# Second attention stage of a two-layer kernel: the second of GpSimd's two row gathers is issued behind the three rounding passes

## What is computed

```python
x = x + tanh(g_xattn[0]) * L0_xattn(layernorm(x), ctx)   # 8 heads of 64
x = x + tanh(g_ffn[0])   * L0_ffn(layernorm(x))          # 16 experts, best 2 of each token
x = x + tanh(g_xattn[1]) * L1_xattn(layernorm(x), ctx)   # 16 heads of 8
x = x + tanh(g_ffn[1])   * L1_ffn(layernorm(x))          # x rounded to fp8, times an fp8 kernel
```

## Time and profile before

| | |
|---|---|
| runs | 1152.71, 1152.83, 1156.85 us, median 1152.83 |
| profiled execution | 1153.63 us, of which the span shown is 1151.9 us |
| busy over the span | PE 90%, PEld 73%, DVE 71%, POOL 56%, ACT 51% |
| stage C | from some 710 us to the end |
| steps 12 to 17 | from 773.16 to 817.47 us |

### The profile page before, as it was taken

The page is one execution under the profiler, slowest core; times in us unless marked ns, Lnnn a source line. Parts: engine busy times, 40 slices in busy tenths (PEclk is TensorE's granted clock), DMA queues, the critical chain, the costliest instruction groups (busy, mean ns, idle before and its releaser), DMA issues. The chain is left out here.

```text
span 1151.9 us, 40516 instructions
## 1 busy us (share of the span) xinstructions
PE 1035.9 (90%) x13498; PEld 844.1 (73%) x13498; DVE 814.5 (71%) x2572; ACT 590.3 (51%) x1415; POOL 650.7 (56%) x1155
## 2 busy tenths in 40 slices
PE   4999999996999997499949996888999999899993
PEld 3787878774777775288848985666788888788882
DVE  1777777776777775655525555577899999799984
ACT  2666666662666564144515442234556555465554
POOL 1333333232777777566663545447777777577656
PEclk9999999997999999599979998799999999899997
DMA  3412112331334300144424543111111111111101
GB/s 76 90 42 52 42 38 61 91 75 40 92 95 108 98 25 27 55 139 140 134 74 130 144 137 89 30 30 29 32 38 37 32 37 38 30 37 34 33 24 31
DMA packets 106902, 74.39 MB, mean 65 GB/s; under 512 B 21360, under 2 KB 98288, under 8 KB 106736
## 3 DMA queue, kind: packets, MB, share of 16 engines
q1 hardware_dynamic: 98544, 55.40, 18.5%
q0 software_dynamic: 8192, 16.79, 4.9%
HBM read 38.60 MB, written 33.55 MB: 63 GB/s over the span
## 5 line engine op out<-in xcount | busy, mean ns | idle before, releaser
L678 ACT ACTIVATE arena<-PS 77x512 f32<-77x512 f32 (+4 forms) x736 | 303.9, 439 | 424.7 <-PE PS L1194 288.4
L1194 PE MATMUL PS<-arena 128*32 128x128 f32 (+5 forms) x9488 | 452.0, 292 | 36.6 <-DMA logit_bias<-in_bias 12.7
L1194 PEld LDWEIGHTS PS<-arena 128*32 128x32 f32 (+4 forms) x9488 | 352.5, 147 | 114.4 <-ACT arena L678 29.1
L604 POOL DMA_INDIRECT moe_in<-moe_results,slot x128 | 130.5, 1020 | 129.1 <-PE PS L1194 63.0
L1194 PE MATMUL PS<-w,arena 128*128 x960 | 192.4, 319 | 2.2 <-ACT arena L741 1.2
L524 POOL DMA_INDIRECT moe_rows<-arena x128 | 127.5, 996 | 71.8 <-POOL arena L520 50.3
L539 POOL TENSOR_TENSOR arena<-arena,minus_half 128x2 f32<-128x2 f32 (+1 forms) x70 | 47.5, 679 | 187.9 <-DVE arena L852 165.8
L1194 PEld LDWEIGHTS PS<-w,arena 128*128 128x128 f32 x960 | 135.0, 195 | 19.3 <-issue 6.2
L1075 DVE TENSOR_TENSOR arena<-PS,b_rows 128x256 f32<-128x256 f32 x160 | 67.7, 424 | 72.1 <-PE PS L1194 50.1
L1194 PEld LDWEIGHTS PS<-arena,wk_wq 128*128 128x128 f32 x512 | 80.3, 197 | 45.5 <-issue 43.0
L1087 DVE TENSOR_REDUCE arena<-PS 128x8 f32<-128x616 f32 x128 | 96.3, 794 | 18.4 <-PE PS L1194 13.1
(11 more groups left out here) (149 smaller groups left out, 1648.8 us busy)
## 6 DMA issues: line engine op xcount, KB each, us to landing
moe_rows<-zeros SPq DMA_DIRECT2D x64, 160.0 KB, 2.5
arena<-moe_rows SPq DMA_DIRECT2D x40, 256.0 KB
moe_results<-arena SPq DMA_DIRECT2D x40, 256.0 KB
residual<-in_x SPq DMA_DIRECT2D x64, 64.0 KB
w<-in_W SPq DMA_DIRECT2D x32, 128.0 KB
arena<-in_ctxC SPq DMA_DIRECT2D x64, 64.0 KB
out<-arena SPq DMA_DIRECT2D x64, 64.0 KB, 1.6
arena<-in_ctxT SPq DMA_DIRECT2D x32, 77.0 KB
```

The source lines that it names most:

```text
L604: g.indirect_dma_start(out=gathered(b, k), out_offset=None, in_=ys_flat[b // CB][:, :], in_offset=bass.IndirectOffsetOnAxis(ap=POS[k][:, b ...
L678: A.activation(o, i, ACT.Copy).then_inc(s[done], 1)
L1194: return T.matmul(o, l, r, start=start, stop=stop)
```

## The change

In GpSimd's `step_c` the first gather of a step stays where it is. The second one, where a step has two, goes behind the three rounding passes and ahead of the root.

```diff
                 if gathers_of(t.value):
 
                     wait_free(pool, s["ST_mm"], t.seen(6, 1))
-                for b, k in gathers_of(t.value):
+                for b, k in gathers_of(t.value)[:1]:
                     gather(b, k)
                 if (b := t.at(12)) is not None:
                     p = t.par(12)
...
                     wait_free(pool, s["xqT_mm"], b - 1)
                     g.tensor_tensor(xq4[p], q4, n4, ALU.add).then_inc(s["xq4_made"], 1)
+                for b, k in gathers_of(t.value)[1:]:
+                    gather(b, k)
 
                 one, two = t.at(1), t.at(8)
                 if one is not None or two is not None:
```

## The result

In ten runs each the changed kernel takes 1148.08 us in the median (1143.56 to 1149.69) and the kernel before 1155.34 (1152.71 to 1162.32). The ratio is 0.9927, with a 95% interval of 0.9912 to 0.9942: 0.73% faster, and clear of no change. The profiled execution took 1148.41 us, its span is 1146.7.

What follows compares the result with a forecast made beforehand. A loop of waits with two nearly equal paths, GpSimd's rounding and the attention, bounds steps 12 to 17. Six steps at 36.42 instead of 44.31 us save 7.89, giving a median of 1145.0 us, range 1143.6 to 1149.5.

Steps and rivals of the forecast that it cites:

- two paths of nearly equal length: Steps 12 to 17: GpSimd's gathers and rounding, and the attention up to the reciprocal; the step shortens only if both do.
- The pauses: TensorE's x72 weight loads stand still 0.56 and 0.54 us; blamed on the second gather, expected to go.
- the edge waits: Rival: pauses come with edge waits up to step 17 or something else there, and stay; 1152.7 us, chance 0.15.
- The reciprocal: VectorE's reciprocal of the denominators starts 1.79 us after the x72 group began instead of 3.21, 1.42 us off.
- L650: GpSimd's rounding ends 2.76 us after the first gather instead of 3.99; TensorE's transpose is released 1.23 us earlier.
- The second gather: Steps 12 to 17: starts some 2.9 us after the first, clear of the x72 group, and takes 1.09 us.
- The root: GpSimd's root waits for the moved gather and ends at 4.84 us; VectorE wants it at 5.32, 0.48 to spare.
- S1 costs nothing: Scores S1 on TensorE beside the moved gather: price 0, from 1.48 us with and without a gather.
- ST: TensorE matmuls after S1: bounds 0 and 1.42 us, taken as 0 for the same 32-row form and little overlap.
- The sum: Steps 12 to 17: two at 6.01 and four at 6.10, 36.42 us instead of 44.31, 7.89 us less.
- the main case: Whole kernel: both paths shorten, 5.8 to 8.5 us gained, 1143.6 to 1147 us; chance 0.68.
- the partial gain: Rival: gather partly holds S1's result or ST, 0.56 us a step; 4.5 gained, 1148.4 us, chance 0.13.

Runs made afterwards that it cites:

- only gather behind the passes: Changed kernel, second gather of steps 0 to 11 behind the root, only gather of steps 18 to 61 behind the three passes: 1167.85 us, ratio 1.013.
- rounding first: Kernel before, with the three rounding passes ahead of both gathers in steps 12 to 17: 1153.04 us, beside 1151.33 of the kernel before.
- behind the first pass: Changed kernel, with the second gather of steps 12 to 17 behind the first of the three rounding passes: 1153.31 us.

## Why the prediction was right, point by point

- **What bounds**: two paths of nearly equal length. Shown by the runs that cure one each beside the change, which cures both (6.11 us a step): 7.15 and 7.16 with the group undisturbed, and 7.43 and 7.45 with the rounding early, in the two steps that left the reciprocal where it was.
- **The pauses are the gather's**: shown. They moved with the gathers, don't come with the edge waits, and a gather 0.34 us later leaves none. The rule of the Trainium skill named in the prediction (*SBUF — State Buffer*, "SBUF: two separate sides") names no path from GpSimd's gather to TensorE, and these runs show that there is one, whatever it is.
- **The reciprocal**: 1.81 us forecast as 1.79. **L650**: 2.76 us behind the first gather (784.12 less 781.36), as forecast. **The second gather**: 2.97 us behind the first, forecast 2.9, and 0.97 us long, forecast 1.09. **The root**: ends at 4.70, forecast 4.84.
- **S1 costs nothing**: L1089 starts 0.89 us behind S1's loads (784.45 to 785.34) against 0.87 in step 19 (826.45 to 827.32), so 0.02 us. The prediction's rows for this were weaker than it says. Both were taken at a granted clock of 0.50, and the gather at 719.37 starts 0.06 us after S1's last load (718.79 + 0.52), so beside S1's result and not beside its loads. The reading came true, but these rows had not shown it.
- **ST**: priced at 0 because only the gather's end reaches it. Right here, but the reason beside it, that its 32-row form is immune as S1's is, was wrong: a gather fully beside ST delays its result by 0.4 us.
- **The sum**: 36.42 us forecast, 36.64 measured. I had GpSimd bind in four steps at 6.10 and 6.01 in two. In step 13 it is the attention's path, and GpSimd idles 0.69 us ahead of the next first gather. Only ahead of step 18's is its idle time down to the 0.17 us that I called the gather's own; ahead of the three before it is 0.31 to 0.34. And the base of 6.01 came from steps without edge waits. These cost 0.06 us a step; with them one gather alone takes 6.09. So the forecast 6.10 a step nearly came true for another reason than the root's, and that the sum is off by only 0.22 us is in part luck.
- **The time**: the median fell by 7.3 us, and 0.73% of 1155.34 is 8.4 us; forecast were 7.8 of 1152.83. The time itself, 1148.08 us, was forecast as 1145.0. It lies outside the 1143.6 to 1147 of the main case and next to the 1148.4 of the partial gain. That isn't the partial gain come true: no pause of 0.5 us is left, and the six steps gained 7.67 us. The forecast started from three runs of the kernel before with a median of 1152.83, and the ten runs have 1155.34, 2.5 us more. Only the wider range held this.

## What to carry to other kernels

An indirect DMA issued by GpSimd is not only GpSimd's time: look at what TensorE is in the middle of, and measure the gather's place in tenths of a microsecond, since 0.34 us decided over 1.4 here. Where two paths are equally long, an edit that shortens one shows nothing, so pick the place that shortens both. And moving a gather also moves what stood behind it: the passes that came forward slowed VectorE, or let the gather slip back into the group.

## What the runs showed of the hardware

How long the group's results were held, in us behind the group's first weight load. The gather given is the last one that starts before the reciprocal does:

| kernel | gather starts | reciprocal starts | between |
|---|---|---|---|
| one gather | 0.17 | 1.79 | 1.62 |
| only gather behind the passes | 1.36 | 2.64 | 1.28 |
| before | 1.62 | 3.21 | 1.59 |
| rounding first, step 13 | 2.19 | 3.72 | 1.53 |

Where the second gather starts at 1.96 (behind the first pass) or 3.15 (the change), the reciprocal starts at 1.80 and 1.81. So in these rows the results of matmuls in progress when a gather starts came no sooner than 1.3 to 1.6 us after its start, and a next gather that starts before that adds its own. At 1.62 the second gather came just before the release at 1.8, at 1.96 just behind it: that would be why 0.34 us decided over 1.4. In the run behind the passes the edge for a lone gather lay at some 1.35 to 1.42 us.

The rule isn't exact. In the run with the rounding first, steps 12, 15 and 16 have their second gathers at 2.52, 2.57 and 2.57 us, and the reciprocals at 3.24, 3.26 and 4.02: 0.72, 0.69 and 1.45 us later. In the first two the result came much sooner behind the second gather than in any row of the table, and no run says why.

That this is a hold on the results, and not slower matmuls, is argued from the weight loads, which in most cases run on without a pause for 24 to 48 of them, and for all 72 where the only gather stands behind the passes. Whether the results themselves or only the signal that they are there came late, these runs can't tell: the reciprocal waits for a semaphore. Which part of the chip passes it on stays open, as does why S1's result is not held beside the same gather: in the changed kernel it was read 1.01 us behind the gather's start (784.33 to 785.34). Whether the writing of descriptors or something else in the gather does it was not tried.
